# One block in place of twelve around the query compression of an attention and mixture layer on eight cores

## What is computed

```python
# x: (4, 2048, 4096); H=4096, QR=1536, NH=32, QK=192, KVR=512
h   = layernorm(x)
q_c = rmsnorm(h @ w_qa, g_qa)          # the stage of the change
q   = (q_c @ w_qb) ...                 # heads, rope on 64 of 192
kv  = h @ w_kva ; k_c = rmsnorm(kv[..., :512], g_kva)
kst = (k_c @ w_kvb) ...
att = softmax(query @ key_s.T * scaling) @ v
x   = x + layernorm(att @ w_o)
x   = x + layernorm(x' @ W_base.T + b_base + lora(x'))   # x' = layernorm(x)
```

## Time and profile before

| | us |
|---|---|
| median of the two timed runs | 4708.9 |
| the two runs | 4666.19 and 4751.6 |
| the profiled execution's own time | 4671.11 |
| its span (core 3, the slowest) | 4669.6 |
| spans of all eight cores | 4640.7 to 4669.6 |
| the four blocks of the first loop, core 3 | 466.6 to 687 |
| the eight blocks of the second loop, core 3 | 687 to 789.7 |
| first matmul of the attention, core 3 | 813.5 |

### The profile page before, as it was taken

The page is one execution under the profiler, slowest core; times in us unless marked ns, Lnnn a source line. Parts: engine busy times, 40 slices in busy tenths (PEclk is TensorE's granted clock), DMA queues, the critical chain, the costliest instruction groups (busy, mean ns, idle before and its releaser), DMA issues. The chain is left out here.

```text
span 4669.6 us, 43267 instructions; the slowest of 8 cores (4640.7 to 4669.6 us)
## 1 busy us (share of the span) xinstructions
PE 3466.5 (74%) x16282; PEld 1360.2 (29%) x16282; DVE 910.3 (19%) x2334; ACT 1332.4 (29%) x1958; POOL 66.6 (1%) x129
## 2 busy tenths in 40 slices
PE   2663771888888888888889888869999138844883
PEld 1332440322222223232232222214444023312331
DVE  3663004111111111111111111100000330024002
ACT  2331000343444444444444344330000230013001
POOL 0000000000000000000000000000000000000000
PEclk9776885988888889888889888889999559976986
DMA  5223111000000000000000000023332326641653
GB/s 145 91 109 55 35 20 30 15 1 15 15 15 15 1 15 15 15 15 15 1 15 15 15 15 1 1 45 64 72 72 54 119 44 109 117 112 35 113 109 108
DMA packets 31370, 218.96 MB, mean 47 GB/s; under 512 B 3888, under 2 KB 4160, under 8 KB 14784
## 3 DMA queue, kind: packets, MB, share of 16 engines
q0 software_dynamic: 17776, 147.97, 17.1%
q1 hardware_dynamic: 13392, 68.24, 3.9%
HBM read 347.37 MB, written 16.78 MB: 78 GB/s over the span
## 5 line engine op out<-in xcount | busy, mean ns | idle before, releaser
L69 ACT ACTIVATE pool<-sPP,pool 128x512 bf16<-128x512 f32 x1024 | 700.0, 687 | 592.9 <-PE sPP L69 592.5
L69 PE MATMUL sPP<-pool 128*128 128x512 bf16 (+1 forms) x2048 | 785.0, 418 | 2.8 <-DVE pool L69 2.8
L69 PE MATMUL PEp<-pool 128*128 128x128 bf16 (+2 forms) x3872 | 590.0, 307 | 149.5 <-DVE pool L69 78.1
L69 PE MATMUL PDq<-pool 128*1 128x512 bf16 (+3 forms) x1792 | 508.6, 347 | 171.5 <-DVE pool L69 118.4
L69 PE MATMUL fP<-pool 128*128 128x512 bf16 (+1 forms) x2176 | 521.7, 398 | 77.6 <-DMA pool<-wbt 40.3
L69 PE MATMUL oP<-pool 128*128 128x512 bf16 x2048 | 457.8, 388 | 57.1 <-ACT pool L69 31.1
L69 DVE BATCH_NORM_STATS2 pool<-pool 128x6 f32<-128x512 bf16 (+1 forms) x344 | 209.4, 676 | 1386.3 <-ACT pool L69 1042.8
L69 PE MATMUL PCq<-pool 128*128 128x512 bf16 x1024 | 431.8, 422 | 0.0
L69 PEld LDWEIGHTS PEp<-pool 128*128 128x128 bf16 (+1 forms) x3872 | 298.8, 100 | 443.9 <-issue 289.4
L69 ACT ACT_TABLE_LOAD x77 | 98.8, 1283 | 1133.7 <-PE PEp L69 359.1
L69 DVE COPY pool<-PDq 1x1024 f32<-1x1024 f32 x64 | 78.0, 1218 | 1430.8 <-PEq L1205 1390.5
(11 more groups left out here) (58 smaller groups left out, 1057.9 us busy)
## 6 DMA issues: line engine op xcount, KB each, us to landing
pool<-wbt POOLq DMA_DIRECT2D x64, 1024.0 KB, 8.7
pool<-xb SPq DMA_DIRECT2D x24, 2048.0 KB, 8.4
pool<-wo POOLq DMA_DIRECT2D x16, 2048.0 KB, 13.1
pool<-wqb POOLq DMA_DIRECT2D x16, 1152.0 KB, 9.8
out<-pool SPq DMA_DIRECT2D x64, 256.0 KB, 2.1
pool<-wqa POOLq DMA_DIRECT2D x4, 3072.0 KB, 22.2
pool<-wkvb POOLq DMA_DIRECT2D x16, 512.0 KB, 11.7
pool<-wkva POOLq DMA_DIRECT2D x1, 4608.0 KB, 32.6
```

The lines of the kernel that those rows point to most:

```text
L69: r = a(*args, **kw)
```

## The change

The twelve blocks become one. The `with` is moved out of the first loop and holds both loops; the two old ones become `if True:`, so that the depth of the code under them stays. No instruction of the computation, no token and no wait on one is added, removed or put in another order on its engine; what goes are eleven block ends, each a drain of all engines and a barrier, and one end is left behind the second loop. From here on lines are one higher: 659 becomes 657, 664 becomes 665, 692 becomes 693, 756 becomes 757.

```diff
-    for sb in range(nqb):
+    with nc.Block() as blk:
+      for sb in range(nqb):
         par = sb % 2
-        with nc.Block() as blk:
+        if True:
             eS0 = sigS.count
...
-    for ti in range(QT):
+      for ti in range(QT):
         par = ti % 2
-        with nc.Block() as blk:
+        if True:
             @blk.vector
```

## The result

| us | before | after |
|---|---|---|
| median of all executions | 4784.0 (10 runs) | 4608.76 (11 runs) |
| lowest | 4662.21 | 4604.2 |
| profiled execution, own time | 4671.11 | 4626.4 |
| spans of the eight cores | 4640.7 to 4669.6 | 4577.4 to 4624.9 |
| ratio to before | | 0.9881, 95% interval 0.9862 to 0.9900 |

The medians compare mixtures, since in some executions of every version here the cores of one die or both had a lower mean granted clock (0.73 to 0.83 in place of 0.84) and the time was 1 to 9% longer, and the ratio, which leaves those out, is the result. It says 1.2% faster: 47 to 64 us of 4665. One more execution of the kernel after, of 4653.18 us, is on record and stands outside the 11.

The account below looks back on a forecast made before the run. PE was taken to wait at block ends for POOL's drain until its just-issued load landed, and for DVE before transposes. Terms of 43.6, 4.6, 9.7, 0.5 and 2.7 us sum to 61.1, so 4671.1 becomes 4610 us; range 4590 to 4680.

Parts of the forecast that it names:

- The barriers between quarters: First loop: three barrier waits of PE, 45.4 us in all, shrink to 0.6 us each; gain 43.6 us.
- The clock behind the holes: First loop: without 22 us holes, second and third quarters run at full clock like the fourth; gain 4.6 us.
- The first chain: Second loop: DVE's tile 0 chain runs beside fourth-quarter matmuls; gain 9.7 us, plus 0.5 us for transposes at full clock.
- The seven barriers between tiles: Second loop: DVE's 3.1 us idle ahead of the next chains falls to 0.4 us; gain 2.7 us.
- The sum: Both loops, on core 3, the slowest: 43.6 + 4.6 + 9.7 + 0.5 + 2.7 = 61.1 us gained.
- The capped clock: Rival, four quarters without rests: chip lowers the clock, giving back 25 us (4635 us), or 39 us at 13/16 (4649); chance 0.07.
- The load that bounds the quarter: Rival, first loop: PE still waits for loads, 4614 us, or no gain there, 4658 us; chance 0.05.
- The rival on the other side: Attention's granted clock settles lower: 0.023 lower loses the whole gain, 0.03 lower gives 4689 us; chance 0.05.

Follow-up runs that it names:

- The run with all barriers kept: Kernel before with all twelve blocks; POOL issues the third and fourth quarters' loads at the start of the next block; ratio 0.9900, profiled execution 4624.62 us.

## Why the prediction was right or wrong

The mechanism was right, point for point, and the time came near: 4610 us were predicted, and six executions of the changed kernel took 4604 to 4609. What was not right is the time before from which this change was counted, and with it the size of the change that a reader would take from the medians.

- **The barriers between quarters.** 43.6 us predicted for core 3; the waits are 2.1 us in place of 45.4 on it, 43.3. The new wait was put at 0.6 us and is 0.71, by 0.1 us for each of three. The run with all barriers kept shows that it is POOL's drain behind a load, and the one with a wait put back shows the same hole made by a semaphore.
- **The clock behind the holes.** 4.6 us predicted on core 3. All later quarters take 41.76 us on all cores, so the term was right there. The first quarter on core 3 was 44.51 in place of 44.00, a small thing that the sum had kept fixed.
- **The first chain.** 9.7 and 0.5 us predicted. The idle time of 9.77 us ahead of the first transposes is gone and they begin 0.16 us before the last matmul's modelled end, 9.9 us; they took 0.83 us in place of 1.44, which is 0.6. The chain started at 603.82 us on core 0; 603 had been predicted for core 3.
- **The seven barriers between tiles.** 2.7 us predicted, 3.8 measured. The step of the sum was that DVE's idle time of 0.39 us is all that a barrier costs. The step fell from 12.74 to 12.25, by 0.49: without the drain DVE's next statistics start at 641.36 us while the last of the copies is still counted until 639.05 + 2.39 = 641.44, so the two overlap by 0.08 us. The three longer steps of before make up the remainder. The term was undersized by over a quarter, 1.1 us.
- **The sum.** 61.1 us predicted for core 3. On it the attention started at 753.3 us in place of 813.5, 60.2 us earlier, but it had started the stretch 1.4 us later. Over the cores the mean is 58.8, since core 3 had one of the longest first loops, 219.3 us against a mean of 216.8. Summing on the slowest core of one profile takes the largest case for all; by itself this is 2 us.
- **How the profiled execution stands to the median.** Here is the step that failed. The prediction took its 61.1 us from the profiled execution's 4671.1, noted that the median of the two timed runs, 4708.9 us, lies 38 us above it, and left that standing. But a predicted 4610 beside 4708.9 is a fall of 2.1%, beside the 4784.0 of ten runs one of 3.6%, and what the edit does is 1.2%. The ten runs of the kernel before show why: four took 4662.2 to 4668.0 us, the other six 4751.6 to 4884.4, so 4751.6 is no measure of this kernel beside 4610. Against 4665, 61 us are 1.3%, and the interval of 0.9862 to 0.9900 just holds it. The difference of 85 us between the two runs was counted into the range's upper end, and should have been taken out of the comparison: it belongs to the executions and not to either kernel.
- **Luck in the 4610.** The four runs of 4662.2 to 4668.0 have a median of 4665.6 us, the like ones of the changed kernel 4607.4, a gain of 58.2. The prediction began 5.5 us too high and took off 2.9 us too much, and the two errors partly cancel.

The rivals. The capped clock did not come in the profiled execution: in the windows of 600 to 630 us, in the dense fourth quarter, all eight cores were granted 1.00; that of core 0 (us, PE busy, PEclk, DMA share, GB/s):

```profile
600.00:630.00 30.00, 30.00 (x187) 1.00 0.01 1
```

That refutes it for this execution. By the Trainium skill (TensorE: Matmul & The Clock Gate, the note on the peak-current limiter) it should have been 13/16; the trace disagrees. But the cap did come in other profiles of this study. The third quarter of the run with DVE's chains ahead, on core 0 and on core 2, two answers:

```profile
551.45 41.76 PE L69 MATMUL qP<-pool 128*128 128x384 bf16 x256 [0.71 <-ACT pool L69]
```

```profile
571.65 50.57 PE L69 MATMUL qP<-pool 128*128 128x384 bf16 x256 [0.71 <-ACT pool L69]
```

Core 0 was granted 1.00 in this quarter and core 2, on the same die, 0.81, which is 13/16. Cores 2 and 3 had it through the whole first loop, which took 206 us on them and 172 on cores 0 and 1. The run with the wait for the landing has the same on cores 6 and 7 (fourth quarter 50.57 us), with its holes of 20 us between the quarters. So the rival's price is real, 34 us; the long stretch is not needed for it, and what sets it off is not shown.

The load that bounds the quarter did not come either, 20.9 us of drain lie under 41.76 us of matmuls. The rival on the other side, a slower attention, is seen only as the scatter of 14 us in the rest, with both signs.

## What to carry to other kernels

In this kernel a block end is as long as the longest thing that any engine still has to drain, and for the engine that issues the loads this is a load's whole way to its landing (21.3 us at the longest behind one load of 3 MB, 41.2 behind the two of the block at line 648, 0.05 behind none). So ask of every barrier what was issued just ahead of it; moving the issue behind the barrier gains nearly as much as removing the barrier (44 of 45 us here), and bare barriers are worth about half a microsecond each (1.3 us for three, 3.8 for seven). Where a dependent chain lies bare, look at what stands before it in its engine's queue: DVE's copies, which wait for PE, stood ahead of chains that need nobody, and this cost 40 us here.

## What the runs showed that was not expected

- DVE's operations overlap a little where no drain stands between them: the statistics start 0.08 us before the end of the twelve copies, and a barrier therefore costs 0.49 us where its idle row says 0.39.
- Loads issued together delay the first of them little: from its issue to PE's start the first of two (3072 KB) took 21.6 us on the mean of the cores, against 20.6 for one alone. What the block end costs there is the wait for the last of them.
- Two cores of a die can be granted 0.81 while the other two have 1.00 in the same loop (the run with DVE's chains ahead, cores 2 and 3 against 0 and 1).
- These matmuls don't feel a load beside them: 0.162 us each with the DMA engines at 0.83, 0.161 without.
